# Second attention of a two-layer block on one core: transposed scores in 18 full banks, ten mask products, maxima rows at the head of each slot, value products dealt to equal rounds

## The reference, cut to what matters

```python
def _L1_attn_ref(x, Wq, bq, Wk, bk, Wv, bv, Wo, bo):
    NUM_HEAD, HEAD_DIM = 16, 16
    q = split_heads(x @ Wq + bq)
    k = split_heads(x @ Wk + bk)
    v = split_heads(x @ Wv + bv)
    attn = jnp.einsum('bhqd,bhkd->bhqk', q, k) / jnp.sqrt(jnp.float32(HEAD_DIM))
    alibi = -slopes[:, None, None] * (Tx - 1 - jnp.arange(Tx, dtype=jnp.float32))[None, None, :]
    attn = attn + alibi
    attn = jnp.where(causal, attn, jnp.finfo(jnp.float32).min)
    p = jax.nn.softmax(attn, axis=-1)
    out = jnp.einsum('bhqk,bhkd->bhqd', p, v).transpose(0, 2, 1, 3).reshape(Bx, Tx, C)
    return out @ Wo + bo
```

## Time and profile before

| | |
|---|---|
| profiled execution, time | 1746.33 us |
| its span | 1744.5 us |
| median of three runs | 1747.72 us |
| PE busy | 1638.5 us (94%) |
| DVE, ACT, POOL busy | 1138.3, 945.4 and 582.1 us |
| mean granted TensorE clock | 0.979 |
| busy on PE, a pass (L885) and t pass (L914) | 136.7 and 133.5 us |

### The profile page before, as it was taken

One profiled execution on the slowest core, in us unless ns is written; L12 is line 12 of the kernel. 1 busy time (PEld: TensorE's weight loads), 2 busy tenths in 40 slices (PEclk: granted clock), 3 DMA queues, 4 the chain that ended last, 5 costly groups with the idle time before them and its releaser, 6 DMA issues.

```text
span 1744.5 us, 33715 instructions
## 1 busy us (share of the span) xinstructions
PE 1638.5 (94%) x11020; PEld 1416.4 (81%) x11020; DVE 1138.3 (65%) x2654; ACT 945.4 (54%) x2038; POOL 582.1 (33%) x518
## 2 busy tenths in 40 slices
PE   4999999999898999899989999999989989998998
PEld 3888989889787677688878888898988867767887
DVE  6666767676535778455776676676756477755557
ACT  3566565555444677543356655656554437773443
POOL 2554444454460102112126355444455320030120
PEclk8999999999899999999999999999999989999999
DMA  4100000000110423101010000000001132211110
GB/s 127 40 26 16 25 1 15 24 16 1 46 57 18 71 43 69 49 28 46 10 51 27 15 16 25 15 24 0 17 3 62 39 58 51 46 51 43 37 46 25
DMA packets 35216, 60.21 MB, mean 35 GB/s; under 512 B 7988, under 2 KB 22068, under 8 KB 33768
## 3 DMA queue, kind: packets, MB, share of 16 engines
q1 hardware_dynamic: 35064, 58.28, 12.5%
HBM read 42.24 MB, written 3.42 MB: 26 GB/s over the span
## 4 chain that ended last, share of the span: by engine, by line
PE 70%; DVE 11%; ACT 7%; issue 7%; POOL 2%; SPq 1%; DMA 1%; DVEq 0%; ACTq 0%; POOLq 0%
PE ps L345 17%; PE ps L347 16%; PE ps L346 16%; PE ps L914 5%; PE ps L885 5%; PE ps L934 4%; ACT E L1121 3%; DVE nmax L1433 3%; PE ps L746 2%; POOL E L1758 1%; ACT PT_h L1103 1%; DVE On L1375 1%; PE ps L917 1%; PE ps L685 1%; PE ps L900 1%
## 5 line engine op out<-in xcount | busy, mean ns | idle before, releaser
L1121 ACT ACTIVATE E<-ps,nmax 128x128 f32<-128x128 f32 (+7 forms) x256 | 189.0, 741 | 206.9 <-DVE nmax L1433 206.3
L1755 POOL TENSOR_SCALAR E<-E,mixc 128x128 f32<-128x128 f32 (+7 forms) x128 | 97.3, 760 | 380.1 <-DVE mixc L1403 380.1
L1229 ACT ACTIVATE PT<-ps 128x512 f32<-128x512 f32 (+3 forms) x384 | 166.2, 494 | 61.5 <-PE ps L917 50.8
L1433 DVE TENSOR_REDUCE nmax<-ps 128x1 f32<-128x128 f32 (+7 forms) x256 | 182.9, 749 | 12.9 <-PE ps L723 12.9
L1758 POOL TENSOR_TENSOR E<-E 128x128 f32<-128x128 f32 (+7 forms) x128 | 182.4, 1425 | 10.7
L1741 POOL TENSOR_TENSOR Fw_l<-Fw_raw,Fw_h 128x768 fp32r<-128x768 f32 x48 | 88.9, 1851 | 258.8 <-ACT Fw_h L1168 258.0
L345 PE MATMUL ps<-V_h,PT_h 128*128 128x256 f32 x576 | 169.3, 294 | 0.0
L346 PE MATMUL ps<-V_l,PT_h 128*128 128x256 f32 x576 | 164.7, 286 | 0.0
L347 PE MATMUL ps<-V_h,PT_l 128*128 128x256 f32 x576 | 164.7, 286 | 0.0
L345 PE MATMUL ps<-XT_h,Fw_h 128*128 128x512 f32 x384 | 155.3, 405 | 8.8 <-DVE XT_l L1306 8.8
L1476 DVE TENSOR_TENSOR Hf<-ps,silu_g 128x512 f32<-128x512 f32 x96 | 66.3, 691 | 136.8 <-PE ps L347 134.7
(11 more groups left out here) (211 smaller groups left out, 4683.2 us busy)
## 6 DMA issues: line engine op xcount, KB each, us to landing
Fw_raw<-in_fa SPq DMA_DIRECT2D x48, 256.0 KB, 2.6
Wa_raw<-in_wa SPq DMA_DIRECT2D x9, 1024.0 KB, 4.9
Wo_raw<-in_wo SPq DMA_DIRECT2D x8, 512.0 KB, 3.5
Fw_raw<-in_fb SPq DMA_DIRECT2D x32, 128.0 KB, 2.6
KS<-QK_h SPq DMA_DIRECT2D x56, 64.0 KB
QS<-QK_h SPq DMA_DIRECT2D x56, 64.0 KB
Xn<-in_x SPq DMA_DIRECT2D x3, 1024.0 KB, 6.0
Fw_raw<-w2s SPq DMA_DIRECT2D x16, 128.0 KB, 2.8
```

What stands on the lines that cost most here:

```text
L1121: nc.scalar.activation(e[:, 0:w], ps[m][:, 0:w], ACT.Exp, bias=nmax[:, s % 4, m:m + 1], accum_out=lsum[:, s % 4, m:m + 1]).then_inc(exp_do ...
L1229: nc.scalar.activation(PT[:, PT_AT[p, n]:PT_AT[p, n] + z - a], bank1(RING1 + n % RING1)[:, at:], ACT.Exp, scale=SCALE1).then_inc(t_used, 1)
L1433: nc.vector.tensor_reduce(nmax[:, s % 4, m:m + 1], ps[m][:, 0:(s % NT + 1) * P], AX.X, ALU.max, negate=True).then_inc(nmax_ready[m], 1)
L1755: nc.gpsimd.tensor_scalar(e2, e2, mixc[:, n % 4:n % 4 + 1], 1.0, ALU.mult, ALU.mult).then_inc(mix_scaled, 1)
```

## The change

It touches the second attention's t pass, its value products, the rows of a slot and the order; the a pass, the number of columns and the number of score products (24 for a pair) are as before.

- The 24 transposed pieces become 18 that each fill a bank of 512 columns. A piece of kind f or a is one product; one of kind b holds two block rows of the same head (384 and 128 columns); one of kind c holds the same block row of both heads (256 and 256). ACT so does 18 exponentials of 512 columns for a pair.
- The 16 mask products of 128 columns become 10: four of 128 columns, and six of 256 whose output is two blocks of the bank, with ident_r read twice.
- The rounds of the value products are dealt anew: the eight products of 128 columns fall into two rounds, the fourth and the tenth, four in each.
- The rows of maxima and ones come to partitions 0 to 3 of a slot, the data to 4 to 51. `nmax1_cols` is 66 columns wide, not 128, and so is its transposed product.
- PT's places become 12 slots of 512 columns. The order string is written anew; n0 moves from the middle of the slot to its end. The second half's maxima are first waited for at t4, before at t1.

```diff
-LOW_K1 = 48
+DATA_ROW, LOW_ROW = 4, 36
-PIECES1 = 24
+PIECES1, TURNED1 = 24, 18
-MAX_ROW = 32
+MAX_ROW = 0
+MAX_COLS = SLOT1 + 2
...
-    nmax1_cols = sb("nmax1_cols", [P, NT, P], F32R, s)
+    nmax1_cols = sb("nmax1_cols", [P, NT, MAX_COLS], F32R, s)
...
-        order = """a0 a1 t0 a2 a3 w4 a4 c0 a5 t1 a6 t2 a7 t3 a8 t4 a9 o0 t5 a10 v0 t6 m0 t7 a11 t8 a12
+        order = """a0 a1 t0 a2 a3 w4 a4 a5 c0 t1 a6 a7 t2 a8 t3 a9 a10 t4 t5 o0 a11 t6 t7 a12 t8 a13 v0 a14
...
-    def t_piece(j):
-        kb, n, half = (j // 4, j // 2 % 2, j % 2) if j < 16 else (4 + (j - 16) // 2, j % 2, 1)
-        return n, kb, half, max(half * HALF, kb * P), (half + 1) * HALF
+    def turned(name):
+        kind, i, n = name[0], int(name[1]), int(name[2:] or 0)
+        a, z = i * HALF, (i + 1) * HALF
+        if kind == "f":
+            return [(n, i, HALF, T)]
+        if kind == "a":
+            return [(n, 4 * i, a, z)]
+        if kind == "b":
+            return [(n, 4 * i + 1, a + P, z), (n, 4 * i + 3, a + 3 * P, z)]
+        return [(n, 4 * i + 2, a + 2 * P, z) for n in range(2)]
+
+    T_PIECES = [turned(name) for name in
+                "a00 a01 b00 b01 f00 f01 c0 f10 f11 f20 f21 f30 f31 a10 a11 b10 b11 c1".split()]
...
-            todo = [(kb, n, q) for kb in range(NT) for n, q in ((0, c), (1, 3 - c)) if kb <= 2 * q + 1]
-            found.append((c, *todo[r]))
+    def v_rounds(c):
+        if c in (0, 3):
+            n = 0 if c == 0 else 1
+            return [(0, n, 0), *((kb, 1 - n, 3) for kb in range(2)), (1, n, 0), *((kb, 1 - n, 3) for kb in range(2, NT))]
+        n = c - 1
+        return [*((kb, n, 1) for kb in range(4)), *((kb, 1 - n, 2) for kb in range(6))]
...
-                for row, src in ((at, QK_h), (at + D1, QK_h), (at + LOW_K1, QK_l)):
+                for row, src in ((at + DATA_ROW, QK_h), (at + DATA_ROW + D1, QK_h), (at + LOW_ROW, QK_l)):
...
-                mm = nc.tensor.transpose(bank1(7)[:, tile(i)], nmax1_cols[:, 4 * half + i, :].bitcast(F32), ident[:])
+                mm = nc.tensor.transpose(bank1(7)[0:MAX_COLS, tile(i)], nmax1_cols[:, 4 * half + i, :].bitcast(F32), ident[:])
...
-                n, kb, half, a, z = t_piece(j)
-                if j in (0, 1, 3):
-                    pe.wait_ge(n_done, 4 * G + (1, 3, 3, 4)[j])
+                level = n_level(j)
+                if j == 0 or level > max(n_level(i) for i in range(j)):
+                    pe.wait_ge(n_done, 4 * G + level)
...
-                bank, base = bank1(RING1 + j % RING1), z - HALF
-                mm = nc.tensor.matmul(bank[:, a - base:], KS[:, p % K_PAIRS, tile(kb)], QS[:, 2 * (p % Q_PAIRS) + n, a:z],
-                                      start=True, stop=True)
-                if a == kb * P:
-                    mm = nc.tensor.matmul(bank[:, a - base:a - base + P], mask_r[:], ident_r[:], start=False, stop=True,
-                                          skip_group_check=True)
+                bank, at, diagonal = bank1(RING1 + j % RING1), 0, []
+                for n, kb, a, z in T_PIECES[j]:
+                    mm = nc.tensor.matmul(bank[:, at:at + z - a], KS[:, p % K_PAIRS, tile(kb)],
+                                          QS[:, 2 * (p % Q_PAIRS) + n, a:z], start=at == 0, stop=True, skip_group_check=True)
+                    if a == kb * P:
+                        diagonal.append(at // P)
+                    at += z - a
+                if diagonal:
+                    blocks = bank.rearrange("p (k c) -> p k c", c=P)[:, diagonal[0]:diagonal[-1] + 1:max(1, diagonal[-1])]
+                    mm = nc.tensor.matmul(blocks, mask_r[:], ident_r[:].unsqueeze(1).to_broadcast([P, len(diagonal), P]),
+                                          start=False, stop=True, skip_group_check=True)
                 mm.then_inc(t_ready, 1)
...
-                    nc.scalar.activation(PT[:, PT_AT[p, n]:PT_AT[p, n] + z - a], bank1(RING1 + n % RING1)[:, at:], ACT.Exp,
+                    nc.scalar.activation(PT[:, at:at + HALF], bank1(RING1 + n % RING1), ACT.Exp,
```

More of the change, by code:

```diff
@@ L399, in slot1 @@
     def slot1(p):
-        order = """a0 a1 t0 a2 a3 w4 a4 c0 a5 t1 a6 t2 a7 t3 a8 t4 a9 o0 t5 a10 v0 t6 m0 t7 a11 t8 a12
-                   t9 a13 t10 a14 n0 a15 t11 t12 t13 a16 a17 v1 a18 t14 a19 t15 a20 t16 a21 t17 t18 a22
-                   a23 t19 v2 t20 v3 t21 m1 t22 t23 n1""".split()
+        order = """a0 a1 t0 a2 a3 w4 a4 a5 c0 t1 a6 a7 t2 a8 t3 a9 a10 t4 t5 o0 a11 t6 t7 a12 t8 a13 v0 a14
+                   a15 t9 a16 v1 m0 t10 t11 a17 a18 a19 t12 t13 t14 a20 a21 v2 a22 t15 t16 a23 n0 t17 m1 v3
+                   n1""".split()
         tokens = [(x.rstrip("0123456789"), int(x.lstrip("abcdefghijklmnopqrstuvwxyz"))) for x in order]
@@ L470, in v_group @@
-    def v_group(k):
[L472 to L489, removed]
+    def turned(name):
[8 more added lines that the diff above has]
+        return [(n, 4 * i + 2, a + 2 * P, z) for n in range(2)]
@@ new lines, in program @@
+    T_PIECES = [turned(name) for name in
+                "a00 a01 b00 b01 f00 f01 c0 f10 f11 f20 f21 f30 f31 a10 a11 b10 b11 c1".split()]
+    assert len(T_PIECES) == TURNED1
+    T_AT = {}
+    for j, piece in enumerate(T_PIECES):
+        at = 0
+        for n, kb, a, z in piece:
+            T_AT.update(((n, kb, q), (j, at + q * 2 * P - a)) for q in range(a // (2 * P), z // (2 * P)))
+            at += z - a
[5 more added lines that the diff above has]
+        return [*((kb, n, 1) for kb in range(4)), *((kb, 1 - n, 2) for kb in range(6))]
@@ new lines, in v_group, with v_needs, pt_free, pt_slot @@
+    def v_group(k):
+        return [(r, c, *v_rounds(c)[r]) for r in range(k * ROUNDS_V, (k + 1) * ROUNDS_V) for c in range(4)]
+    def v_needs(k):
+        return {T_AT[n, kb, q][0] for r, c, kb, n, q in v_group(k)}
+    V_LAST = [max(k for k in range(GROUPS_V) if j in v_needs(k)) for j in range(TURNED1)]
+    PT_SLOTS = PT_COLS // HALF
+    def pt_free(p, j):
+        g = TURNED1 * p + j - PT_SLOTS
+        return None if g < 0 else GROUPS_V * (g // TURNED1) + V_LAST[g % TURNED1]
+    def pt_slot(p, j):
+        return (TURNED1 * p + j) % PT_SLOTS * HALF
@@ L492, in program, with n_level @@
+    def n_level(j):
+        return max(2 * (a // HALF) + n + 1 for n, kb, a, z in T_PIECES[j])
     LN_B = 4 * NT
@@ L551, in load_query_rows @@
                 at, heads = h % 2 * SLOT1, slice(h % 8 * D1, h % 8 * D1 + D1)
-                for row, src in ((at, QK_h), (at + D1, QK_l), (at + LOW_K1, QK_h)):
+                for row, src in ((at + DATA_ROW, QK_h), (at + DATA_ROW + D1, QK_l), (at + LOW_ROW, QK_h)):
                     sp.dma_start(QS[row:row + D1, 2 * slot + h % 2, cols].bitcast(F32),
@@ L923, in weigh_values @@
                 G = PAIRS1 * b + p
-                last = max(T_INDEX[n, kb, q // 2] for c, kb, n, q in v_group(k))
-                pe.wait_ge(t_used, PIECES1 * G + last + 1 + RING1)
+                pe.wait_ge(t_used, TURNED1 * G + max(v_needs(k)) + 1 + RING1)
                 if k == 0:
@@ L929, in weigh_values @@
                     pe.wait_ge(vb_done, NT * b + NT)
-                for c, kb, n, q in v_group(k):
+                for r, c, kb, n, q in v_group(k):
                     cut = P if kb == 2 * q + 1 else 0
-                    j = T_INDEX[n, kb, q // 2]
-                    at = PT_AT[p, j] + q * 2 * P - t_piece(j)[3]
+                    j, off = T_AT[n, kb, q]
+                    at = pt_slot(p, j) + off
                     mm = nc.tensor.matmul(bank1(6)[32 * c:32 * c + 32, n * 2 * P + cut:(n + 1) * 2 * P],
-                                          Vs[:, kb, 2 * p + n, :], PT[:, at + cut:at + 2 * P], start=kb == 0 and n == 0, stop=True,
+                                          Vs[:, kb, 2 * p + n, :], PT[:, at + cut:at + 2 * P], start=r == 0, stop=True,
                                           skip_group_check=True, tile_position=(0, 32 * c))
```

21 lines of the change are left out of this document (8 added, 13 removed).

## The result

Six runs of the changed kernel took 1735.57 to 1739.21 us, median 1737.49; six of the kernel before 1746.45 to 1751.79, median 1748.11. The ratio is 0.9946, with a 95% interval of 0.9928 to 0.9964: about 9.4 us less. The profiled executions took 1737.75 us (span 1735.9) and 1746.33 (span 1744.5), 8.6 us apart. Their mean granted clocks of TensorE are alike, 0.982 and 0.979.

A forecast was written before the change was run, and what follows sets the result against it. Steady slots were taken as bound by PE's work, last slots by the PE-ACT hand-over. Per batch -3.0 - 0.25 - 1.65 = -4.9, for both -9.8 from 1746.33: 1736.5, median 1737.9 us, range 1731.5 to 1745.

The forecast's parts named there:

- Value products, -0.22: Second attention: a round lasts as long as its widest product, so one more group takes 0.78 us: -0.22 us a slot.
- Masks, -0.54: Transposed score pass: six fewer mask products at 0.11 us each, six wider ones 0.02 more each: -0.54 us a slot.
- Transposes, 0: Transposed maxima at 66 columns: the streamed 128 columns set the length, so no gain was taken.
- Added waits, +0.26: Steady slot: new waits on ACT at t14 and on DVE around a20 to a23, charged +0.26 us a slot.
- The end of a slot: n1 needs a23's maximum, m1 and the transposes; DVE is in time if it starts a23 at once, a little late otherwise.
- The slower rival: At the slot's end DVE lags by more than one maximum, so PE stands at n1: 1755 us, chance 8%.
- Last slots: End of a batch: the last steady slot loses 0.50 us, the last slot 1.65 through less PE work and fewer hand-overs.
- The walk's end: Stepping through the last slot from w4 gave 11.3 us; half the rest taken, about 12.4 in place of 13.97.
- First slot, -0.25: First slot of a batch: PE is not its limit all the way, so half the steady gain counts, -0.25 us.
- The sum for a batch: Six steady slots -3.0, first slot -0.25, last slot -1.65: -4.9 us a batch, -9.8 for both.
- the four terms for the steady slot: Value products -0.22, masks -0.54, transposes 0, added waits +0.26: -0.50 us a steady slot.

The follow-up runs named there:

- experiment 3: Changed kernel with each diagonal block's mask product apart again, 16 of 128 columns in place of ten: steady slots 17.54 to 17.77 us, whole 1743.32 us.
- experiment 7: Changed kernel with only a new alternating order string (steady slots 16.74 to 16.80, 1735.11 us), or with four value groups and new orders (1727.42 and 1727.36 us).
- experiment 5: Changed kernel with n0 moved back to the slot's middle, behind a18 instead of a23: steady slots 17.75 to 18.09 us, 0.65 us longer.

## Why the prediction was right, and where its steps were not

The mechanism was right as a whole: steady slots are bound by PE's own products, the last ones also by the hand-over to ACT, and both got shorter. 1737.9 us was predicted, 1737.49 measured. Step by step:

- **Value products, -0.22:** measured -0.21 in the group and -0.19 in the slot. The reason was wrong: not the widest product of a round, but the strip with the most columns in the group.
- **Masks, -0.54:** measured -0.43. The term was over-sized: I charged every load in full. Four of the six products were worth about 0.10 each, the one ahead of a value group 0.06, and the last one before the outputs nothing.
- **Transposes, 0:** measured 0.
- **Added waits, +0.26:** this step failed. It began with the earlier trace rows, which I read as waits of the t pass for ACT and of the a pass for DVE; 6.1 of their 7.0 us are the idling ahead of the loads directly behind value groups. And halving the exponentials and the plain maxima returns at most 0.07 us. Yet the slot shrank by only 0.46 (17.59 to 17.13), not by 0.21 + 0.43 = 0.64. The other 0.18 is in PE's own sequence: with split masks, experiment 3 stands at 17.56, hardly under the 17.59 of before, although v1 is 0.21 shorter. Where it lies can be read from the starts of PE's products in the third to fifth slot. From one start to the next, the t pass with its masks takes 6.26 us a slot before and in experiment 3, the value products 4.79 and 4.58, the a pass 5.45 and 5.62. So it is in the a pass, whose products did not change. In the kernel before, three of a slot's five groups stood behind a product of 128 columns, two of them a mask, as here:

```profile
614.24 0.22 PE L917 MATMUL ps<-ident_r,mask_r 128*128 128x128 f32 x1
614.39 1.07 PE L934 MATMUL ps<-PT,Vs 128*32 128x256 f32 x16
```

That product takes 0.15 us there, and the other two groups stand behind a pieces of 512 columns. Now four groups stand behind a pieces of 512 columns, each of which costs at least 0.10 more there than between wide products. That these two more are the cause is argued, not shown; that the order alone can move twice as much (0.36) is shown by experiment 7. What of the 0.18 belongs to the order and what to the packing into 18 banks stays open. The old dealing of the rounds under the new pieces was not tried.
- **The end of a slot:** I named the chain over DVE and m1 as the risk, with n1 waiting for it. n1 runs on behind v3 with no wait of its own: ACT's copies of n0 end 0.06 us before v3 does, and the maxima are there. The slower rival did not occur; experiment 5 shows that such a queue behind n0 on ACT can cost 0.65 us a slot.
- **Last slots:** predicted -0.5 and -1.65, together -2.15; measured -2.03 and -1.89. The walk's end (12.4 us) was right to 0.1. How it is spread was wrong: the sixth interval did not lose 0.5 (16.72 to 16.79), the last one lost 2.10. The sixth hangs on DVE's and ACT's work: with halved maxima it takes 15.88, with halved exponentials 16.14.
- **First slot, -0.25:** measured 42.09 to 42.06 us from the first a product to the first output, and 42.67 to 42.83 in the second batch: nothing. This stretch took 40.1 to 44.6 us among the kernels tried, at a mean granted clock of 0.91 in the shortest and 0.85 in the longest (here 0.88 in both kernels in the first batch, 0.84 before and 0.88 after in the second); the steady slots have 1.00. So it is no place to read a gain of 0.2 from.

The sum for a batch was -4.9 and came out at -4.2 and -4.1. The profiled pair, from which the sum was made, says -8.6 us where -9.8 was predicted: 1.2 us too much. That the medians, 10.6 apart, hide this is chance. Two of the four terms for the steady slot were wrong, 0.11 us too much for the masks and a charge for waits that stood for something else, and they nearly cancelled.

## What to carry to other kernels

Where an engine is the bound, the total wait of its weight loads does not tell what the path loses. Look at what stands ahead of each load (here, mostly a value group), then halve the work of the engine waited for and look at the interval. And do not price an instruction by the distance to the next start alone, but split it or leave it out: the ten masks took 1.25 us by their distances, and leaving them out gave 0.48, since neighbours and waits took the rest. When the instructions are fixed, the order of wide and narrow products, and how often PE turns to the value groups, is worth as much as removing a few.

## What the runs showed of the hardware

- Products in four strips of 32 columns do not keep step. A group with uneven rounds but equal strips takes the same 0.79 us; a strip with two wide products makes it 0.98.
- A value group has a price at each edge: a 512-column product directly ahead of it or directly behind it takes 0.33 us instead of 0.23. A slot with one group less (and another order) was 0.14 us shorter beyond the groups' own time.
- The first weight load behind a value group starts together with its product (640.60 both), not under what stands ahead, as loads between other products do (640.94 for the product at 641.17). It comes after 0.41 us of idling behind a wide group and 0.20 behind a narrow one (v1, w4), with the maxima and exponentials halved as without, and the waits view names DVE, ACT or nothing for it.
- A float32 transpose takes 276 ns in its record and 0.11 us from start to start with 66 columns of weights as with 128; only its load record is shorter (112 ns against 140).
